# A new order for the attention stage: two tiles in flight, and a conditioning chain that moves by one step

## What is computed

```
x = x + attn(cond(x))           # first part: the "attention stage"
x = x + ffn(gru(cond_2048, x))  # second part: 32 recurrent steps

cond(x):  blocks = x.reshape(B, 8, 4, H).sum(2)        # eight block sums per sequence
          keys   = rmsnorm(blocks @ Wk.T) * rms_weight
          a      = softmax(keys @ q)                   # weights of the eight blocks
          y      = x + (a @ blocks) @ Wo.T             # the same row added to every token
          return layernorm(y) * gamma + beta
attn(y):  q, k, v = split(y @ W_attn + b)              # 32 heads of width 8
          p = softmax(mask(q k / sqrt(8) + alibi))     # causal, 32 x 32 for each head
          return (p v) @ W_proj + b_proj
gru:      h = (1 - z) * tanh(i_n + r * h_n) + z * h    # for each of the 32 tokens
```

## Time and profile before

| | us |
|---|---|
| median of 3 runs | 506.21 (505.97 to 507.7) |
| the profiled execution: its time | 506.46 |
| the profiled execution: span from first to last instruction | 504.4 |
| head, up to the first `transpose_y(1)` | 56.9 |
| one loop pass (a group), 56.87 to 91.39, 91.39 to 125.73, ... | 34.5, 34.3, 34.3, 34.3 |
| attention after the loop, up to the last `project_out` | 228.6 to 318.7 |
| recurrent part | from 318.7 on |

### The profile page before, as it was taken

How to read it: one execution, slowest core, us unless ns; L and a number is a source line. 1 busy time by engine, 2 the same in 40 slices (tenths; PEclk the granted TensorE clock), 3 DMA queues, 4 the chain that set the end, 5 groups by cost and what they waited for, 6 DMA issues and landing times.

```text
span 504.4 us, 13154 instructions
## 1 busy us (share of the span) xinstructions
PE 468.7 (93%) x4962; PEld 406.6 (81%) x4962; DVE 359.6 (71%) x1049; ACT 242.1 (48%) x584; POOL 49.6 (10%) x67
## 2 busy tenths in 40 slices
PE   7489899999999999999989978799999999999995
PEld 5258688797888897988878867788999999999994
DVE  3814689698797897896877688456767677676675
ACT  1252554836557547457465625344444444444341
POOL 7321201201202112012012000000000000000000
PEclk9969999999999999999999999999999999999999
DMA  8515443454433444433432330000001010010101
GB/s 304 206 51 156 133 125 97 132 129 118 146 98 110 141 107 150 122 93 114 108 107 67 99 106 6 3 0 2 21 22 43 2 42 22 21 44 1 42 22 64
DMA packets 81863, 42.59 MB, mean 84 GB/s; under 512 B 53793, under 2 KB 74913, under 8 KB 81825
## 3 DMA queue, kind: packets, MB, share of 16 engines
q1 hardware_dynamic: 81824, 42.07, 28.3%
HBM read 25.28 MB, written 16.78 MB: 83 GB/s over the span
## 4 chain that ended last, share of the span: by engine, by line
PE 65%; DVE 11%; ACT 6%; issue 5%; POOL 3%; DMA 2%; SPq 2%; POOLq 0%; DVEq 0%; ACTq 0%
PE ps_s L1090 6%; PE ps_s L1257 6%; PE ps_t L1257 6%; PE ps_o L1257 5%; PE ps_t L1102 5%; PE ps_s L1229 5%; PE ps_a L1044 4%; PE ps_t L1229 4%; PE ps_a L1053 4%; PE ps_m L1131 4%; PE ps_a L1229 4%; PE ps_m L1229 3%; POOL yT_r L452 3%; PE ps_a L1019 3%; DVE mx L774 3%
## 5 line engine op out<-in xcount | busy, mean ns | idle before, releaser
L1090 PE MATMUL ps_s<-kbd,qbd 128*128 128x128 f32 x512 | 65.7, 282 | 0.0
L535 ACT ACTIVATE sc<-sc 128x512 f32<-128x512 f32 x64 | 38.8, 628 | 54.4 <-DVE sc L778 54.4
L766 DVE COPY_PREDICATED masked<-kst,ps_s 128x512 f32<-128x512 int32 x64 | 46.8, 741 | 24.1 <-issue 20.0
L1090 PEld LDWEIGHTS ps_s<-kbd,qbd 128*128 128x128 f32 x512 | 62.9, 196 | 0.1
L1044 PE MATMUL ps_a<-yT_r,w_qkv_r 128*128 128x512 f32 x192 | 53.3, 422 | 2.6 <-ACT yT_r L498 1.5
L1044 PEld LDWEIGHTS ps_a<-yT_r,w_qkv_r 128*128 128x128 f32 x192 | 35.7, 196 | 14.4 <-POOL yT_r L452 4.9
L778 DVE TENSOR_TENSOR sc<-masked,mx 128x512 f32<-128x512 f32 x64 | 41.0, 680 | 0.0
L774 DVE TENSOR_REDUCE mx<-masked 128x16 f32<-128x512 f32 x64 | 40.4, 671 | 0.0
L1102 PE MATMUL ps_t<-kst,sc 128*128 128x128 f32 x256 | 35.2, 277 | 4.6 <-ACT sc L535 4.6
L631 ACT ACTIVATE zg<-ps_t,brz 128x128 f32<-128x128 f32 x64 | 20.0, 364 | 38.8 <-PE ps_t L1257 38.8
L911 DVE SCALAR_TENSOR_TENSOR rg<-ps_o,vec,rg 128x128 f32<-128x128 f32 x64 | 19.5, 346 | 26.8 <-PE ps_o L1257 22.9
(11 more groups left out here) (108 smaller groups left out, 844.7 us busy)
## 6 DMA issues: line engine op xcount, KB each, us to landing
xf<-in_x_feat SPq DMA_DIRECT2D x8, 512.0 KB, 4.0
xg<-in_x_tok SPq DMA_DIRECT2D x8, 512.0 KB, 4.5
q_dram<-qn SPq DMA_DIRECT2D x16, 256.0 KB, 3.1
k_dram<-kn SPq DMA_DIRECT2D x16, 256.0 KB, 2.9
qbd<-q_dram SPq DMA_DIRECT2D x64, 64.0 KB, 2.4
kbd<-k_dram SPq DMA_DIRECT2D x64, 64.0 KB, 2.2
v_dram<-vn SPq DMA_DIRECT2D x16, 256.0 KB, 2.5
vbd<-v_dram SPq DMA_DIRECT2D x64, 64.0 KB, 2.0
```

The lines of the kernel that those rows point to most:

```text
L535: nc.scalar.activation(part, part, ACT.Exp).then_inc(sc_exp, 1)
L766: nc.vector.copy_predicated(kept, keep.unsqueeze(1).to_broadcast([P, NH // 2, S]), ps_s[:, h * 512:(h + 1) * 512].rearrange("p (h k) -> p ...
L1090: last = nc.tensor.matmul(bank[:, q * P:(q + 1) * P], tile_q[:, i % TH, :], kbd[:, :, i // TH, h * HW + q, cols], start=True, stop=True)
```

## The change

PE, DVE and ACT get a new `tile_step(g, i)`. SP and POOL stay as they are. The hardware loops of PE, DVE and ACT become Python loops, so that all 8 groups are written out with one step function, and the special code for group 7 goes.

In the step of tile `n` the engines now do `scores(n+1)`, then the end of tile `n-1` (`transpose_attn`, `project_out`, `normalise`, `residual`), and in the middle of tile `n` `transpose_probs(n)`. `probs_v(n)` comes last on PE. Before, the step ended with `transpose_probs(n+1)`, and all of `n` was done in it. On DVE, `softmax_shift` is cut into `softmax_max` and `softmax_shift`, and `add_proj` loses the statistics to `token_stats`, so that pieces of the conditioning chain can stand between them. `cond_row`, `cond_col`, `spread_proj` and `add_proj` come one step earlier than before. `block_sums` goes from step 1 to the end of step 3. The block products stay in step 3.

```diff
             # PE
-            def tile_step(g, i, norm_ahead, cond_ahead):
+            def tile_step(g, i):
                 n = GT * g + i
-                if i == 0:
+                last_group, norm_ahead = g + 1 == NG, g + 2 < NG
+                if i == 0 and not last_group:
                     transpose_y(g + 1, norm_ahead)
-                scores(n + 1, g + (i + 1) // GT, (i + 1) % GT)
+                if n + 1 < NT:
+                    scores(n + 1, (n + 1) // GT, (n + 1) % GT)
+                if n > 0:
+                    transpose_attn(n - 1)
+                transpose_probs(n, n % 2, first=(n == 0))
+                if n > 0:
+                    project_out(n - 1)
                 if norm_ahead and i == 1:
-                    cond_row(g + 2)
-                if norm_ahead and i == 2:
                     cond_col(g + 2)
-                if i == 2:
+                if i < 3 and not last_group:
                     work_ahead(g + 1, i, 0)
                     work_ahead(g + 1, i, 1)
...
+                if norm_ahead and i == 0:
+                    cond_row(g + 2)
+                if g + 3 < NG and i == 3:
+                    pe.wait_ge(v_out, 2 * g + 4)
+                    block_products(g + 3, ps_a[:, 0:512])
+                if norm_ahead and i == 1:
                     pe.wait_ge(ra_ready, g + 3)
                 probs_v(n, g, i)
-                if norm_ahead and i == 2:
-                    pe.wait_ge(v_out, 2 * g + 4)
+                if norm_ahead and i == 1:
+                    pe.wait_ge(k_out, 2 * g + 4)
                     spread_proj(g + 2)
...
             # DVE
-            def tile_step(g, i, norm_ahead, cond_ahead):
+            def tile_step(g, i):
                 n = GT * g + i
...
+                if n > 0:
+                    normalise(n - 1)
+                if norm_ahead and i == 1:
+                    cond_shift(g + 2)
+                if n + 1 < NT:
+                    softmax_mask(n + 1, (n + 1) % 2)
...
+                if n + 1 < NT:
+                    softmax_max(n + 1, (n + 1) % 2)
...
+                if n + 1 < NT:
+                    softmax_shift(n + 1, (n + 1) % 2)
...
-                if cond_ahead and i == 1:
-                    block_sums(g + 3, l_xf, DMA * (g + 1))
...
+                if n > 0:
+                    residual(n - 1, (n - 1) // GT, (n - 1) % GT)
+                if norm_ahead and i == 1:
+                    add_proj(g + 2)
+                if g + 3 < NG and i == 3:
+                    block_sums(g + 3, l_xf, DMA * (g + 1))
             # ACT
...
+                if n > 0:
+                    attn_out(n - 1)
+                probs_out(n)
...
+                if i == 3 and g + 2 < NG:
+                    normalise_tokens(g + 2)
+                if n + 1 < NT:
+                    softmax_exp(n + 1, (n + 1) % 2)
+                if i == 3 and g + 3 < NG:
                     cond_out(g + 3, ps_a[:, 0:512])
```

More of the change, by code:

```diff
@@ L598, in tile_step @@
[L598 to L602, removed]
-                for i in range(GT):
[L604 to L620, removed]
-                if i + 1 < GT:
-                    probs_out(n + i + 1)
-                if i + 2 < GT:
-                    softmax_exp(n + i + 2, i % 2)
+                if i == 3 and g + 2 < NG:
[3 more added lines that the diff above has]
+                if i == 3 and g + 3 < NG:
+                    cond_out(g + 3, ps_a[:, 0:512])
@@ new lines, in tile_step @@
+                if g == NG - 2 and i <= C:
+                    if i == 0:
+                        act.wait_ge(wqkv_lo, 3)
+                        act.wait_ge(w_ready, 2)
+                    if i < C:
+                        copy_out(w_ih_r[0][:, i, :], w_ih[:, i, :]).then_inc(w_hi, 1)
+                    else:
+                        copy_out(w_f_r[0][:, :, :], w_f[:, :, :]).then_inc(w_hi, 1)
+            for g in range(NG):
+                for i in range(GT):
+                    tile_step(g, i)
@@ L626, in gates @@
+            attn_out(NT - 1)
             def gates(t):
@@ L1198, in tile_step @@
-                transpose_attn(n)
-                if cond_ahead and i == 3:
-                    block_product(g + 3, ps_a[:, 0:512], 1)
-                if i == 3:
-                    project_out(n)
-                transpose_probs(n + 1, (i + 1) % 2)
-                if i < 3:
-                    project_out(n)
-            with pe.Fori(0, NG - 3) as g:
-                for i in range(GT):
-                    tile_step(g, i, True, True)
-            for g in (NG - 3, NG - 2):
-                for i in range(GT):
-                    tile_step(g, i, g < NG - 2, False)
@@ L1214, in _ @@
-            g, n = NG - 1, GT * (NG - 1)
-            scores(n + 1, g, 1)
-            for i in range(GT):
-                probs_v(n + i, g, i)
-                if i + 2 < GT:
-                    scores(n + i + 2, g, i + 2)
-                transpose_attn(n + i)
-                if i + 1 < GT:
-                    transpose_probs(n + i + 1, (i + 1) % 2)
-                project_out(n + i)
+            for g in range(NG):
+                for i in range(GT):
+                    tile_step(g, i)
@@ L1225, in exact_product @@
+            transpose_attn(NT - 1)
+            project_out(NT - 1)
             def exact_product(dst, w_r, col, rhs_r, first=True):
```

94 lines of the change are left out of this document (32 added, 62 removed).

## The result

| | before | after |
|---|---|---|
| median of the runs of one comparison, us | 506.09 (4 runs, 505.28 to 507.7) | 527.07 (4 runs, 525.84 to 529.11) |
| ratio, 95% interval | | 1.0414 (1.0367 to 1.0462) |
| the profiled execution, us | 506.46 | 529.11 |
| mean granted clock of that execution | 0.988 | 0.959 |

A run more than 1.5% above the fastest of its kernel counts as slow and is left out of the ratios, though not of the medians and ranges; this concerns four of ten runs of one experiment, two of ten of another and one of ten of a third.

What follows compares the result with a forecast made beforehand. PE's instruction list was taken to bound the loop. Five passes with the first's saving +14.8, group 5 -1.8 and last tiles -1.8 sum to +11.2 us; from 506.2 this gives 517.4, forecast as 517.0 us, range 511 to 526.

Steps and rivals of the forecast that it cites:

- What bounds the kernel: Loop: PE's instruction list sets the pass, 33.3 us of work; the new order can win about 1 us per pass.
- The step with the block products: Step 3, all five passes: PE stands 4.0 us for DVE's late block sums; the step takes 10.7 us instead of 7.42.
- The products end at 9.9, `probs_v` at 10.7: Step 3, behind the stall: end times of block products and probs_v, in us from the start of scores.
- The other steps: Steps 0, 1 and 2 of a pass: 9.0, 10.1 and 7.8 us, within a pass taken as 37.5 us.
- The first pass: First loop pass: step 0 has no tile n-1 and saves 1.2 us, losing none of its start.
- Group 5, group 6, last tiles: After the loop: group 5 -1.8 us, probs_v(28) unchanged at 35.4 us, from there to the last project_out -1.8 us.
- The third: Rival: the clock falls in each step 3 stall, slowing the work behind by 2 to 5 us; about 529 us, 14%.
- The first rival: Step 3: block sums don't hold PE, but cond_out holds the next transpose_y; pass 34.8 us, total 504 us, 6%.
- the second's: Rival: waits for block sums and cond_out both vanish in step 3; pass 33.4 us, total 497 us, 4%.
- The fourth rival: Written-out code is fetched more, costing 1 us for a group; total 522 us, 5%.

Runs made afterwards that it cites:

- the filled stall: Changed kernel plus eight unread 128x256 products ahead of the block products in step 3, filling PE's wait: 520.22 us, ratio 1.0254.
- the last attempt: Changed kernel with sums two steps earlier, cond_out before exponentials, input loads earlier, plus unread products in two gaps and last group's value save earlier: 505.57 us, 0.996.
- the third stall kernel: Changed kernel with block sums between masks and maxima of step 3, and cond_out ahead of the exponentials: 507.84 us, ratio 1.0022.

## Why the prediction missed, point by point

**What bounds the kernel**: right. PE's list sets the pass, and the stall went in at full length.

**The step with the block products**: right in place, cause and size of the wait. 4.0 us were forecast and 3.92 to 3.94 measured, and the products start 8.06 us after `scores` where 8.05 was forecast. That it fits to 0.01 us is luck: the second mask came 0.2 us later than in the sum, and the pieces behind it were as much shorter. The term "The products end at 9.9, `probs_v` at 10.7" is the step that failed: it prices the work behind the stall at full clock. It is right for the kernel with the filled stall (2.72 us to `transpose_y`), and 1.4 to 2.2 us too low in each pass of the kernel after.

**The other steps**: right. A pass of 37.5 was forecast, and the filled stall shows 37.4 to 37.5 from the second pass on. One small wait was overlooked: `cond_row` waits 0.3 to 0.5 us for DVE's `cs` in each step 0. Except in the first pass, it is within the small terms.

**The first pass**: the 1.2 us that it was to save aren't there. With the filled stall it takes 37.96 us, no less than the others. `transpose_attn` and `project_out` are missing in its step 0, but `cond_row` stands behind them and waits for DVE's `cs`, which is ready no earlier. The forecast had left that wait out. Against it the head is 0.6 us shorter: `transpose_probs(0)` used to lie in the gap ahead of `transpose_y(1)`. Now PE is idle there for 2.66 us, and in this execution the clock fell behind it: `scores` at 57.18 takes 3.33 us instead of 2.05. The pass lost 0.24 us by that, as the last attempt shows.

**Group 5, group 6, last tiles**: -1.8, 0 and -1.8 were forecast, -1.7, +0.3 and -1.6 measured. The wait for `vbd` is still there (0.40 us at 322.87).

**The rivals.** The third happened as it was described, in all five passes of the profiled execution: "about 529 at 2.4 us" for each against 527.1 and 2.0. It had 14%. The mis-sized term goes back to the argument for that chance: "The new stall is just shorter, 3.9 us", and "no stretch of that length is in the trace". The nearest row was the 4.54 us with a clock of 0.50 behind it, and nothing in the trace spoke for a limit between 3.9 and 4.5. Taken by its nearest row, the fallen clock belonged in the sum: at the lower end of that rival's own price, 2 us, it is 517 + 10. The range left out "the larger half of the clock's" and so missed by 1 us. Even 2.04 us of idleness were enough four times in five. The section of the Trainium skill's "TensorE: Matmul & The Clock Gate" named "HAM oscillation — how this bites in real kernels" describes a loop of this kind: matmuls with a wait in each trip of the loop, and the work behind each wait starts at the low clock. The trace agrees, with 0.50 behind each of five stalls.

The first rival's pass of 34.8 was 34.2 in the run that makes it, and the second's 33.4 was 33.4. Their times, 504 and 497, were too low for the medians (509.0 and 509.6), since the prediction took SP's chain as unchanged and it becomes late in the new order. The fourth rival's 1 us for each group was not seen, nor a wait for code. Writing out costs 1.5 us in all (0.29% of 507.04, interval 0.02 to 0.56%), in the profiled execution through late transfers.

## What to carry to other kernels

Ask of each producer that an in-order engine waits for where it stands in *its* engine's step: at the end of DVE's step, 2 us of sums cost PE 4 us each time, and two steps earlier nothing. Price an idle stretch of TensorE as idle time plus what the clock takes from the work behind it (here 1.2 to 2.2 us for stalls of 2 to 4 us, in 14 of 15 stalls), and if the trace has only one row near that length, take its outcome as the forecast. And before paying for an idle stretch or a fallen clock, look whether PE would wait for something else right behind it: then it is worth less than its row says. When the order of the compute side changes, look next at what the DMA queue starts just ahead of its urgent transfer.

## What the runs showed of the hardware

**The clock falls in or behind shorter gaps than expected, and not always for the same one.** The gap of 2.66 us in the head is the same in eight of these kernels. Behind it `scores` took 3.33 to 3.52 us in four profiled executions and 2.05 in the other four. The 3.16 us wait of the third stall kernel had no fall behind it (2.15 us for `scores` at 156.23), and neither had the 2.76 us wait of the kernel before with early inputs (the query products behind it take 3.04 us), while 2.03, 1.95 and 2.04 us did elsewhere. The gap of 2.12 us ahead of `transpose_attn(30)`, the same in eleven of the twelve kernels, has a fall behind it in six and none in five. So the length of a gap alone does not decide it, and what else does was not found out. "TensorE: Matmul & The Clock Gate" in the Trainium skill says, in "What's actually happening", that the monitor's time base runs freely and does not start with the kernel, so that the point of change varies. The two outcomes of the same 2.66 us agree with it.

**A save behind two loads of 512 KB took 5.2 to 7.8 us from its start to the load that waits for it, instead of 3.8**, when the second of these loads was started 0.6 to 1.4 us ahead of it in the same queue (seven saves of two transfers of 256 KB, in the passes of four kernels). With 2.2 us or more between them it was 3.8 to 5.2 us. The loads are not the only cause: in the last group, with no input load for over 35 us, it was 5.3 us in the kernel after and 3.9 in the kernel before. What else delays it stays open, and so does why the time differs so much between runs of one kernel (502.6 to 512.9 us), since only one run of each was profiled.
